# The output stage of a graph-transformer layer taken tile by tile, with three gate projections moved behind the recurrence

## The reference

```python
scores = softmax(h @ Wgate); rw, sel = top_k(scores, 2); rw = rw / sum(rw)   # 4 experts, 2 for a token
q, k = l2norm(silu(h @ Wq)), l2norm(silu(h @ Wk)); v = silu(h @ Wv)          # 8 heads of 64
def step(S, x):                       # for each token, in each expert that it uses
    S = S * exp(gt)
    delta = (vt - k_t @ S) * bt
    S = S + outer(k_t, delta)
    return S, (q_t * scale) @ S
_, o = scan(step, S0, xs)
core = einsum('ble,eblhv->blhv', w_full, o)          # both experts' outputs, weighted
gate = silu(h @ Wg)
core = core * rsqrt(mean(core * core, -1) + 1e-5)    # per head
core = core * o_norm_weight * gate
x = x + core.reshape(L, 512) @ Wo
```

## Time and profile before

| | |
|---|---|
| median of three runs | 1015.61 us |
| the profiled execution | 1018.47 us, span 1016.7 us, mean granted clock 0.97 |
| PE busy | 909.4 us (89%) |
| DVE busy | 600.5 us (59%) |
| POOL busy | 370.0 us (36%) |
| ACT busy | 254.0 us (25%) |
| recurrence, first to last matmul | 592.80 to 949.06 us |
| output stage, first transpose to last matmul | 970.03 to 1013.13 us |

### The profile page before, as it was taken

The page is one execution under the profiler, slowest core; times in us unless marked ns, Lnnn a source line. Parts: engine busy times, 40 slices in busy tenths (PEclk is TensorE's granted clock), DMA queues, the critical chain, the costliest instruction groups (busy, mean ns, idle before and its releaser), DMA issues.

```text
span 1016.7 us, 28629 instructions
## 1 busy us (share of the span) xinstructions
PE 909.4 (89%) x12622; PEld 583.9 (57%) x12622; DVE 600.5 (59%) x1297; ACT 254.0 (25%) x500; POOL 370.0 (36%) x303
## 2 busy tenths in 40 slices
PE   3999999988999999999999978889988889798288
PEld 2444444444666444444444458888888788788243
DVE  7799999457888323315545265546555556454274
ACT  1221122010222000023111324333433334343141
POOL 5111100000111300000788557555656464643482
PEclk9999999978999999999999989999999999999789
DMA  8400000000000140000046644434343444321452
GB/s 241 141 0 1 1 1 0 1 0 1 1 1 2 51 178 1 0 1 1 15 176 224 256 140 112 125 97 128 98 127 97 110 112 111 106 69 25 107 152 71
DMA packets 73189, 78.25 MB, mean 77 GB/s; under 512 B 34189, under 2 KB 55847, under 8 KB 73063
## 3 DMA queue, kind: packets, MB, share of 16 engines
q1 hardware_dynamic: 67943, 55.24, 19.4%
q0 software_dynamic: 5120, 21.14, 5.8%
HBM read 51.95 MB, written 24.35 MB: 75 GB/s over the span
## 4 chain that ended last, share of the span: by engine, by line
PE 80%; DVE 9%; issue 6%; POOL 3%; ACT 1%; DMA 1%; SPq 0%; DVEq 0%; POOLq 0%
PE bank L827 16%; PE bank L750 14%; PE bank L759 8%; PE bank L517 7%; PE bank L547 4%; PE bank L533 3%; PE bank L928 2%; PE bank L600 2%; DVE rows L1573 2%; POOL big L1358 2%; PE bank L839 2%; PE bank L904 2%; PE bank L524 2%; PE bank L938 2%; PE bank L942 2%
## 5 line engine op out<-in xcount | busy, mean ns | idle before, releaser
L750 PE MATMUL bank<-W,xT 128*128 128x512 f32 x320 | 138.6, 593 | 0.0
L750 PEld LDWEIGHTS bank<-W,xT 128*128 128x128 f32 x320 | 60.6, 190 | 75.7 <-issue 75.5
L759 PE MATMUL bank<-hs,big 125*125 125x512 f32 x200 | 86.6, 593 | 0.0
L1240 POOL TENSOR_TENSOR big<-big,ident_sb 125x125 f32<-125x125 f32 x10 | 11.4, 1141 | 195.8 <-ACT big L1059 195.8
L517 PE MATMUL bank<-W,xT 128*125 128x512 f32 x160 | 78.6, 610 | 0.0
L827 PE MATMUL bank<-big 64*64 64x64 f32 x1920 | 71.3, 221 | 3.4 <-issue 2.3
L1301 POOL TENSOR_TENSOR tB<-tA,masks_sb 128x512 f16<-128x512 f16 x20 | 39.4, 1968 | 94.0 <-DVE tA L1797 94.0
L827 PE MATMUL bank<-tB 64*64 64x64 f16 x2560 | 61.4, 196 | 11.3 <-issue 6.4
L827 PEld LDWEIGHTS bank<-big 64*64 64x64 f32 x1920 | 64.1, 136 | 4.8 <-issue 3.8
L533 PEld LDWEIGHTS bank<-rows 128*126 128x126 f16 x360 | 44.5, 138 | 35.6 <-issue 24.2
L759 PEld LDWEIGHTS bank<-hs,big 125*125 125x125 f32 x200 | 37.3, 188 | 47.7 <-issue 47.4
(11 more groups left out here) (287 smaller groups left out, 1910.4 us busy)
## 6 DMA issues: line engine op xcount, KB each, us to landing
big<-qkv_slots SPq DMA_DIRECT2D x40, 256.0 KB, 3.8
rows<-step_rows SPq DMA_DIRECT2D x40, 128.0 KB, 3.2
rows<-gam_rows SPq DMA_DIRECT2D x40, 128.0 KB, 3.1
big<-qkv_slots SPq DMA_DIRECT2D x80, 64.0 KB, 2.7
big<-qkv_slots SPq DMA_DIRECT2D x40, 128.0 KB, 2.9
o_slots<-big SPq DMA_DIRECT2D x40, 128.0 KB, 2.6
x_all<-in_x SPq DMA_DIRECT2D x10, 224.0 KB
out<-tC SPq DMA_DIRECT2D x10, 224.0 KB
```

The source lines that it names most:

```text
L750: last = mm(bank[:, b0, :], xT[:, k, t * P:t * P + 128], W[:, w, k, :], start=(k == 0), stop=(k == KC - 1))
L759: last = mm(bank[0:P, t % 2, :], cnt[:, s, t * P:(t + 1) * P], hs[:, s, :], start=(s == 0), stop=(s == NT - 1))
```

## The change

The gate projections of tiles 7, 8 and 9 (`LATE = 7`) are taken out of their place before the recurrence. TensorE does them after its last recurrence step, into PSUM banks 1 to 3; ACT does their Silu there, ahead of its first weighting; VectorE multiplies them by the norm weight one at a time within the output stage. So that their operands live that long, ACT saves two quarters of `xT`'s last 375 columns to `kvbd` and `iota` before the recurrence, and `AT` and `TF` move to free places in `big` and `xT`, since `W[:, 3]` is now needed to the end.

In the output stage each engine has a new written order. POOL takes the power for tiles 0, 1, 8 and 9 singly and for the others in pairs, and gathers in another order. ACT weighs and squares a tile before it weighs the next. VectorE does a tile's mixing and moments together (`token_rows`). TensorE does transposes and product tile by tile for 0, 1, 8, 9, and in pairs for the rest.

```diff
+LATE = 7
@@ buffers
-        AT = [unit(xTu, 6 + s) for s in range(2)]
+        AT = [unit(big, 21), xTu[:, 3 * (N + 3) + 1:3 * (N + 3) + 1 + D].rearrange("p (a n) -> p a n", n=CL)]
-        TF = [[unit(Wu, 12 + 2 * p + s) for s in range(2)] for p in range(2)]
+        TF = [[unit(big, 8 + 11 * p + s) for s in range(2)] for p in range(2)]
+        lateT = [kvbd[:, :, :].rearrange("p c n -> p (c n)"), iota[:, :].bitcast(f32)] + [xT[:, k, LATE * P:N] for k in (2, 3)]
@@ TensorE
-            for t in range(2, NT):
+            for t in range(2, LATE):
                 project_rows(t, 3)
-            pe.wait_ge(S["f_act"], 4 * NT)
+            pe.wait_ge(S["f_act"], feature_count(LATE - 1, 3))
...
+            for t in range(LATE, NT):
+                for k in range(KC):
+                    last = mm(bank[0:P, 1 + t - LATE, :], lateT[k][:, (t - LATE) * P:(t - LATE + 1) * P], W[:, 3, k, :], start=(k == 0), stop=(k == KC - 1))
+                last.then_inc(S["f_psum"], 1)
...
-            for g in range(NT // 2):
-                for t in (2 * g, 2 * g + 1):
-                    gated_columns(t)
-                for t in (2 * g, 2 * g + 1):
-                    out_rows(t)
+            for t in (0, 1):
+                gated_columns(t)
+                out_rows(t)
+            for t in (2, 4, 6):
+                gated_columns(t)
+                gated_columns(t + 1)
+                out_rows(t)
+                out_rows(t + 1)
+            for t in (8, 9):
+                gated_columns(t)
+                out_rows(t)
@@ ACT
-            for t in range(2, NT):
+            for t in range(2, LATE):
                 feature_rows(t, 3)
+            for k in range(2):
+                A(lateT[k][:, 0:N - LATE * P], xT[:, k, LATE * P:N], ACT.Copy)
...
+            for t in range(LATE, NT):
+                act.wait_ge(S["f_psum"], feature_count(t, 3))
+                A(hs[:, t, :].rearrange("p (b j e) -> p b j e", b=2, e=DH), by_halves(1 + t - LATE, P), ACT.Silu).then_inc(S["f_act"], 1)
...
+            def slot_rows(t):
+                weigh(t)
+                square(t)
...
+            for t in (2, 4):
+                keep_columns(t)
+                keep_columns(t + 1)
+                slot_rows(t + 3)
+                if t == 2:
+                    slot_rows(t + 4)
...
@@ POOL
-            def norm_pair(g):
-                pair = nrm[0:P, g % 2 * 2:g % 2 * 2 + 2, 0:H]
-                pool.wait_ge(S["f_ms"], 2 * g + 2)
-                G.tensor_tensor(pair, pair, phalf[0:P, 0:2 * H].rearrange("p (t h) -> p t h", t=2), ALU.pow).then_inc(S["f_rs"], 1)
+            def norm_rows(t, n):
+                some = nrm[0:P, t % 4:t % 4 + n, 0:H]
+                pool.wait_ge(S["f_ms"], t + n)
+                G.tensor_tensor(some, some, phalf[0:P, 0:n * H].rearrange("p (t h) -> p t h", t=n), ALU.pow).then_inc(S["f_rs"], 1)
...
@@ VectorE
-            for t in range(NT):
+            for t in range(LATE):
                 gate_rows(t)
...
+            def token_rows(t):
                 mix_rows(t)
+                moments(t)
+            token_rows(0)
+            token_rows(1)
+            finish(0)
+            token_rows(2)
+            finish(1)
+            token_rows(3)
+            last_sum(dve, V, 0)
+            token_rows(4)
+            last_sum(dve, V, 1)
+            finish(2)
+            finish(3)
+            gate_rows(7)
+            token_rows(5)
+            token_rows(6)
+            finish(4)
+            finish(5)
+            last_sum(dve, V, 2)
+            gate_rows(8)
+            token_rows(7)
+            last_sum(dve, V, 3)
+            finish(6)
+            finish(7)
+            gate_rows(9)
+            token_rows(8)
+            token_rows(9)
+            last_sum(dve, V, 4)
...
```

More of the change, by code:

```diff
@@ L1196, in keep_columns @@
                 A(fT[:, t % 2, 0:KC * P], bank[:, 4 + t % 2, 0:KC * P], ACT.Copy).then_inc(S["fT_done"], 1)
-            for g in range(NT // 2 + 1):
-                if g < NT // 2:
-                    for t in (2 * g, 2 * g + 1):
-                        weigh(t)
-                    for t in (2 * g, 2 * g + 1):
-                        square(t)
-                if g:
-                    for t in (2 * g - 2, 2 * g - 1):
-                        keep_columns(t)
+            def slot_rows(t):
+                weigh(t)
+                square(t)
+            slot_rows(0)
+            slot_rows(1)
+            slot_rows(2)
+            keep_columns(0)
+            slot_rows(3)
+            keep_columns(1)
+            slot_rows(4)
+            for t in (2, 4):
[4 more added lines that the diff above has]
+                    slot_rows(t + 4)
+            keep_columns(6)
+            keep_columns(7)
+            slot_rows(8)
+            slot_rows(9)
+            keep_columns(8)
+            keep_columns(9)
         @block.gpsimd
@@ L1359, in fetch @@
                                          bass.IndirectOffsetOnAxis(ap=posi[:, c, t:t + 1], axis=0)).then_inc(gathered[t % 4], 16)
-            def norm_pair(g):
-                pair = nrm[0:P, g % 2 * 2:g % 2 * 2 + 2, 0:H]
-                pool.wait_ge(S["f_ms"], 2 * g + 2)
-                G.tensor_tensor(pair, pair, phalf[0:P, 0:2 * H].rearrange("p (t h) -> p t h", t=2), ALU.pow).then_inc(S["f_rs"], 1)
-            for t in range(4):
-                fetch(t)
-            for g in range(NT // 2):
-                if 2 * g + 4 < NT:
-                    fetch(2 * g + 4)
-                norm_pair(g)
-                if 2 * g + 5 < NT:
-                    fetch(2 * g + 5)
+            def norm_rows(t, n):
+                some = nrm[0:P, t % 4:t % 4 + n, 0:H]
+                pool.wait_ge(S["f_ms"], t + n)
+                G.tensor_tensor(some, some, phalf[0:P, 0:n * H].rearrange("p (t h) -> p t h", t=n), ALU.pow).then_inc(S["f_rs"], 1)
+            for t in range(3):
+                fetch(t)
+            norm_rows(0, 1)
+            fetch(3)
+            norm_rows(1, 1)
+            for t in (4, 5, 6):
+                fetch(t)
+            norm_rows(2, 2)
+            fetch(7)
+            norm_rows(4, 2)
+            fetch(8)
+            fetch(9)
+            norm_rows(6, 2)
+            norm_rows(8, 1)
+            norm_rows(9, 1)
         @block.vector
@@ L1882, in finish @@
             def finish(t):
-                dve.wait_ge(S["f_rs"], t // 2 + 1)
+                dve.wait_ge(S["f_rs"], t + 1 if t < 2 else t // 2 + 2 if t < NT - 1 else t // 2 + 3)
                 V.tensor_tensor(tt3(got(t, 0)[0:P, :]), tt3(got(t, 0)[0:P, :]), bc(nrm[0:P, t % 4, 0:H], DH),
                                 ALU.mult).then_inc(S["f_gated"], 1)
-            for t in range(2):
+            def token_rows(t):
                 mix_rows(t)
-            for g in range(NT // 2):
-                for t in (2 * g, 2 * g + 1):
-                    moments(t)
-                if g + 1 < NT // 2:
-                    for t in (2 * g + 2, 2 * g + 3):
-                        mix_rows(t)
-                if g:
-                    last_sum(dve, V, 2 * g - 2)
-                for t in (2 * g, 2 * g + 1):
-                    finish(t)
-                if g:
-                    last_sum(dve, V, 2 * g - 1)
-            for t in (NT - 2, NT - 1):
+                moments(t)
[25 more added lines that the diff above has]
+            last_sum(dve, V, 4)
+            finish(8)
+            last_sum(dve, V, 5)
+            finish(9)
+            for t in range(6, NT):
                 last_sum(dve, V, t)
```

## The result

The changed kernel takes 1037.3 us (median of four runs, 1030.64 to 1043.26), the kernel before 1015.71 beside it on the same chip: a ratio of 1.0198, 95% interval 1.016 to 1.0236. The same program, timed again in six runs, gave 1032.65 (ratio 1.0154, 1.012 to 1.0187). So it is slower, as forecast, but by more than the 1028.5 forecast. The first timing lies above the top of the range, 1034, and the second inside it. The profiled execution took 1040.51 us for a span of 1038.7, which is 22.0 longer than before.

A forecast was written before the change was run, and what follows sets the result against it. TensorE was taken to bound the kernel (80% of the span), with POOL also at its limit in the output stage. Tail +12.3, clock +1.5 and start -0.9 gave +12.9: 1028.5 us on the median, range 1020 to 1034.

The forecast's parts named there:

- the tail: From the recurrence's end to the last matmul: end at 1025.4 against 1013.13 on the old clock, +12.3 us.
- the start: Start of the recurrence: 3.3 us gained by waiting for a DMA, 2.4 lost at half clock, 0.9 gained.
- two clock terms: Output stage: some 0.3 us for tile 0's matmuls at half clock, 1.5 (0 to 3) for matmul 6 after its wait.
- Late projections and head: After the recurrence: projections take 10.4 us to 959.4, first transposes at 967.4, first output matmuls end at 973.2.
- Tiles 2 and 3: Output stage: POOL's power for both ends at 980.6, the finish at 981.3, and TensorE waits 3.4 us.
- Tiles 4 and 5: Output stage: TensorE idle 0.7 us before matmul 4 and 1.3 before matmul 5, which waits for tile 3's sum.
- The ring: Matmul 6 waits for tile 4's sum, queued behind tiles 8 and 9, which wait on copies 6 and 7: 7.6 us lost.
- The end: Matmuls 6 and 7 end at 1016.0, then tiles 8 and 9 one by one, to 1025.4 against 1013.13.
- cold throughout: Rival: half clock at 981 and at the recurrence's start, with no gain there; 1032 us, chance 12%.
- The faster-side rivals: Three rivals: TensorE stays fed, 1011, 5%; start gives all 10.4, 1019, 8%; only sum 4's wait counts, 1024.5, 15%.
- The power of one tile: POOL in the output stage: 125x8 taken as 1.66 us, between 1.20 for 125x5 and 1.96 for 125x10.

The follow-up runs named there:

- the one with the wait filled: The changed kernel with seven extra products in TensorE's wait ahead of the recurrence, whose results nobody reads; ratio 1.0112 to the kernel before.
- the kernel with the tail's gap filled: The changed kernel with eight extra products behind the late projections, into a bank nobody reads; ratio 1.019 to the kernel before.
- the new order with nothing filled: Kernel before with late projections and another output order (pairs on TensorE, sums ahead of tiles they would wait for), no added products; ratio 0.9986.
- The three kernels with a filled start: Extra products in the wait ahead of the recurrence: late projections with old output order 0.9947, changed kernel 1.0112, another new order with both waits filled 0.9911.

## Why the prediction was off

The sum was +12.3 for the tail, +1.5 for its clock and -0.9 for the start, +12.9 in all; the span grew by 22.0. Of the 9.1 us between them, 5.9 are in the stretch up to the recurrence's end, which had only the start as a term, and the rest in the tail, mostly in its two clock terms. Point by point, with times counted from the recurrence's end:

- *The start.* Forecast: first transposes released by a DMA at about 589.5, at half clock, 2.4 us lost to it. Seen: 590.56, 1.94 long, and 1.9 lost by the second unit, whose transposes start at 599.06, against 599.43 in the kernel before. Forecast and trace agree up to there (-0.4 for -0.9). What failed is what I took as nothing, the recurrence that follows: it ran 363.5 against 356.3, and the start's account ended at +5.0. In the second profile of the same program the account was +0.2 (949.27 against 949.06), since that one began 2.3 us sooner; its recurrence was long too. In all four profiles with this order and an unfilled start it took 361.0 to 363.7, in the one with the wait filled 353.1. With other output orders and an unfilled start it took 357.9 and 358.8, with this order and no wait there 358.6. So the loss repeats and is gone in the one profile with the wait filled, the half clock of the first two units is 1.9 us of it, and the cause of the rest stays open.
- *Late projections and head.* They end at +10.5 (forecast +10.4), the first transposes start at +18.6 (+18.3). Right. The first product took 6.66 where I had 3.57 and 0.3 for the clock: this step failed. I read the return of the clock as 3.0 us from the one place where it stood; here it was 7.4 after the first transposes. That row was by luck a short one: in the kernel with the new homes alone, whose tail is the old one, the first pair's products took 8.96, not 7.76. The size differs from execution to execution, too: this product took 6.00 in the second profile of the changed kernel and 5.20 in the one with a warm start.
- *Tiles 2 and 3.* Start +33.3 (+32.2), gap 1.45 where I had 3.4. The gap was smaller since TensorE came late from the cold head; without that it was 3.74. The error of the step before was thus mostly absorbed here, which is why the filled gap gained nothing.
- *Tiles 4 and 5.* Gaps 0.82 and 1.37, forecast 0.7 and 1.3. Right; by now 1.7 us behind the forecast in all.
- *The ring.* Gap 8.16, forecast 7.9 (of which 7.6 were called lost), released by VectorE's sum. Right in place, cause and size. The product after it lost 9.93 - 7.13 = 2.8 to the clock, not 1.5: the half of 3.0 us was again too little, since the clock returned 5.4 us after the product's start. The 2.8 lie within the 0 to 3 that were given, and the runs spread over half of that: behind the same wait the product took 9.60 in the second profile, 8.71 with the order only and 8.60 with a warm start.
- *The end.* The last matmul at +81.2, where the sum had 76.3 and 1.5 for the clock, 77.8: 3.4 short, 1.7 from the head up to tile 5, 1.3 from the second clock term, and 0.4 in small terms.

The mis-sized terms are thus the two clock terms and the recurrence, which stood in the sum as unchanged and is the largest of the three. Of the rivals, "cold throughout" comes nearest, at 12% and 1032; but it put 1.5 on half clock at tiles 2 and 3, where the clock was full again (1.00 from 981), and 1.9 on a start without gain, and had nothing for tile 0's product. The faster-side rivals fell: SP's loads, not ACT, released the start, the sum of tile 4 came as worked out, and tiles 2 and 3 waited for POOL, 3.74 us once the head was warm.

The power of one tile, bounded by two other operations, took more than the 1.66 that I had put between them, and the reason is an overlap that the sum did not have. Lines by form of POOL after, 955 us to the end:

```profile
L1392 POOL DMA_INDIRECT big<-o_slots,posi x20 | 20.0, 1000 | 13.4 <-DMA o_slots<-big 8.1 <-issue 5.3
L1398 POOL TENSOR_TENSOR nrm<-nrm,phalf 125x16 f32<-125x16 f32 x3 | 9.5, 3178 | 5.1 <-DVE nrm L1920 5.1
L1398 POOL TENSOR_TENSOR nrm<-nrm,phalf 125x8 f32<-125x8 f32 x4 | 8.0, 1999 | 10.0 <-DVE nrm L1920 9.9
```

A single tile took 2.00, so four singles cost 8.0 where two pairs had cost 6.2. The gathers took 1.00, not 1.11. The rule from the Trainium skill that I weighed (SBUF — State Buffer, "SBUF: two separate sides"), by which a VectorE instruction with two SBUF inputs and a GpSimd one block each other, shows in one direction. On VectorE the multiplication with the gate (L1921) follows the scaling that releases the power, so three of the four single powers began 0.17 us into it, and the fourth inside a mixing; one gather, too, began inside such a multiplication:

```profile
968.03 0.69 DVE L1921 TENSOR_TENSOR big<-big,hs 125x512 f32<-125x512 f32 x1
968.20 2.05 POOL L1398 TENSOR_TENSOR nrm<-nrm,phalf 125x8 f32<-125x8 f32 x1 [2.55 <-DVE nrm L1920]
...
974.64 0.69 DVE L1921 TENSOR_TENSOR big<-big,hs 125x512 f32<-125x512 f32 x1
974.86 1.35 POOL L1392 DMA_INDIRECT big<-o_slots,posi  x1 [0.19 <-issue]
```

In the kernel with the tail's gap filled, tile 1's power began outside:

```profile
971.29 1.67 POOL L1400 TENSOR_TENSOR nrm<-nrm,phalf 125x8 f32<-125x8 f32 x1
```

Over the twelve profiles of this document, 26 of the 32 single powers began while a VectorE instruction with two SBUF inputs ran and took 1.92 to 2.05; the other six took 1.63 to 1.68. Of the 240 gathers, 61 took more than 1.03 us, and every one of these began so (nine of the kernel before's 20 and three of the changed one's, hence the lower mean); none of the 150 that began otherwise took more than 1.02, 46 of which began while VectorE ran an instruction with one SBUF input. So 1.66 was right for a power by itself, and what was missing is the overlap, 0.3 to 0.4. The other direction does not show: VectorE's multiplications that began during a power or a gather took 0.67 to 0.69, as the others did. Nor did the three moved gate products lengthen a gather, since none ran when a gather began. The one at 997.64 (above) began inside a gather and ended ahead of the next:

```profile
997.10 0.96 POOL L1392 DMA_INDIRECT big<-o_slots,posi  x1 [0.30 <-issue]
998.38 0.95 POOL L1392 DMA_INDIRECT big<-o_slots,posi  x1 [0.32 <-issue]
```

## What to carry to other kernels

When an order is rewritten, follow each bank and buffer round its ring: a wait that hangs on an item queued behind the very work it would release (here a sum behind two later tiles) costs a full round trip, and moving one line shows it. A wait of TensorE has a second price, the half clock in the work behind it, and one row of how soon the clock returned is no bound for the next place. If such a wait can't be closed, spare products in it are worth trying, but only where TensorE is what comes late afterwards: they paid at the recurrence's start and, in the changed kernel, nothing in the tail's head. And look at what the other engines run when an instruction is released: here the same instruction that releases POOL's power is followed by one that makes it up to a fifth longer.

## What the hardware showed beyond that

- *The clock's return varies.* From the first work after the wait to the window in which the clock is clearly above half again: 3.0 us before (970.03, the window from 973); 5.4 after the ring in the changed kernel (1015.65, 1021); 6.3 in the new order with nothing filled, whose transposes begin at 966.67 and whose clock is 0.97 from 973; 7.4 in the changed kernel's head (972.63, 980); 10.4 at the changed kernel's recurrence (590.56, 601), where the work was broken by short waits. What tells these apart is not settled. The Trainium skill (TensorE: Matmul & The Clock Gate, HAM oscillation) has as its rule that the engine should have no long idle gaps, since the work behind one starts throttled. The three kernels with a filled start agree: their first transposes took 1.09 against 1.94, and the first two units 1.9 us less.
- *The recurrence's length.* The three profiles with the start's wait filled have 352.0, 353.1 and 354.8 us; the nine without have 356.3 to 363.7, three of them with no such wait at all (356.3, 357.0, 358.6). One profile each, so this is a pattern and not a measured effect. Between the kernel before and the changed one, of TensorE's idle time only the part put down to "issue" grew: gaps of 0.9 us and more were 15 with 20.9 us before, 21 with 26.6 in the changed kernel's first profile, 14 with 19.9 in its second, 14 to 16 with 17.1 to 18.3 in the filled ones. What opens them stays open. The clock is a part of the pattern at most: summed over windows, the recurrence ran at half clock for 3.4 to 6.8 us in the filled ones, 17.1 before, 14.4 and 24.2 in the changed kernel's two profiles, but also only 3.4 with the new homes alone, which took 357.0.
